# Turning half of the q tiles in 32x32 blocks on VectorE and through DRAM, and moving the output's addition and its LayerNorm sums to ScalarE and GpSimd

## The chip, the core and the metric

The kernel runs on one core of a Trainium2 chip. The metric is the device time of one execution in microseconds. A core has five instruction streams that matter here: TensorE (PE in the profile; its weight loads are listed apart as PEld), VectorE (DVE), ScalarE (ACT), GpSimd (POOL) and SyncE (SP), which here only issues DMA transfers. They run side by side and are ordered by semaphores alone: an instruction waits until a counter has reached a value, and everything behind it in its stream waits too.

## What is computed

Sixteen batches of x and ctx, each 128 channels by 1024 positions, in float32. First a linear attention between x and ctx, whose output is added to x, then a feed-forward part with a routed table of values:

```python
x = x + xattn(layernorm(x), ctx, ctx, Wq, Wk, Wv, Wo, bo, g)
x = x + ffn(layernorm(x), ...)

def xattn(q, k, v, ...):              # 8 heads of 64
    qh = softmax(Wq q, over the 64) * 64 ** -0.5
    kh = softmax(Wk k, over the 1024 positions)
    vh = Wv v
    context = einsum('hdn,hen->hde', kh, vh)
    out = Wo einsum('hde,hdn->hen', context, qh) + bo
    return out / max(norm over channels, 1e-12) * g * sqrt(128)
```

LayerNorm runs along the 1024 positions. The FFN part is computed from its sums, so the mean and variance of every row of the new x are needed before it begins.

## The kernel before

**Stages.** The attention stage runs the batches through a pipeline of periods, one batch a period, each of four steps (`for b in range(PERIODS): for i in range(4)`). In the loop, `b` is the batch whose k tiles are made, `p = b - 1` the one whose q tiles are made and whose context product is taken, `o = b - 2` the one whose output is taken, `e = b - 3` the one that is finished. Every engine has the same loop written out in its own block, in an order set by hand. After it comes the FFN stage, whose first steps are woven into the last periods.

**The k side.** `k_tile` (L444) makes four tiles of k with 1024 columns; VectorE takes a maximum (`k_maximum`, L1102), ScalarE the exponential (`k_exponential`, L734). The result has to be turned, so that the context product can contract over positions: VectorE transposes it in 32x32 blocks into `kt` (`k_turn`, L1106), and SP moves the blocks between partitions into `ekT`, in 2 halves of 16 DMAs of 64 KB for each batch (`move_k`, L377, issue in L384). `g_part` (L471) on TensorE waits until a half has landed. In the first batch GpSimd issues half of these DMAs.

**The q side.** `q_pair` (L453) makes four q tiles a batch, each of two groups of 128 positions. VectorE subtracts the maximum of each head (`q_shift`, L1120), ScalarE takes the exponential, VectorE the sums and reciprocals (`q_reciprocal`, L1130), GpSimd scales (`q_scale`, L966). The scaled tile lies in `qs_sb`, with two buffers. TensorE turns all four tiles with eight transpositions each into the PSUM tensor `turn` (`q_turn`, L462), ScalarE copies them to `q_hd` (`q_copy`, L750), and `o_pair` (L495) multiplies them with the batch's matrix `mt_sb`.

**The output.** ScalarE copies the products (`o_copy`), sums their squares (`o_square`), GpSimd scales by the norm (`norm_scale`, L978), TensorE turns the result into `turn` (`o_turn`, L510). VectorE adds it to x in one operation (`residual`, L1141) and takes the row statistics (`statistics`, L1146: two `bn_stats` of 512 columns and an aggregation). GpSimd makes the reciprocal deviation (`rstd2_pow`, L987). `turn` is shared: whoever uses it next on TensorE waits for the copy of the one before (`take_turn`, L615).

**SP's order.** In the loop of L401 SP issues, for batch b: the load of x for b + 1, the first half of `move_k`, the loads of ctxT for b and of ctx for b + 2, the second half of `move_k`. After the loop come the small tables of the FFN stage. Each block of moves waits for the two transposes of its half and for the `g_part` that last read the buffer.

Of the kernel before, what the change touches and what calls it, by code (L numbers as in the profile page):

```python
# [25 lines left out]
MOVED = 16 * QUAD * QUAD  # L26
LN_EPS = 1e-5
# [15 lines left out]
def place(h):  # L43

    return (h % 2) * (H // 2) + h // 2


def attention_ffn_kernel(nc, x, ctx_rows, ctx_cols, WqT_raw, WkT_raw, Wv_rows, WoT_rows, bo_row, g_col, Wuq_cols,
# [3 lines left out]
    with ctx:  # L52
# [19 lines left out]
        q_hd = sb("q_hd", [P, T, N])  # L72
        qs_sb = sb("qs_sb", [P, 2, N])
        mt_sb = sb("mt_sb", [P, 2, T, C])
# [11 lines left out]
        kscale = sb("kscale", [P, T])  # L86
# [4 lines left out]
        mv1 = sb("mv1", [P, 2])  # L91
# [24 lines left out]


# [151 lines left out]
        kscale_done = sem("kscale_done")  # L269
# [14 lines left out]
        q_copied = sem("q_copied")  # L284

# [78 lines left out]
        def _(sp):  # L364
# [22 lines left out]

            sp.dma_start(WkT_in, WkT_raw).then_inc(k_weights_in, 16)
# [22 lines left out]
            for half in range(2):  # L411
                sp.wait_ge(k_moved[half], moved(B))
            sp.dma_start(bu1[:, :], bu1_row.broadcast_to([P, UH])).then_inc(ffn_in, 16)
            sp.wait_ge(q_prod, 4 * B)
            sp.wait_ge(g_prod, 2 * B)
            sp.wait_ge(m_prod, B)
            for src, dst in ((Wu2_row.broadcast_to([P, UH]), Wu2[:, :]),
                             (bu2_row.broadcast_to([P, 1]), bu2[:, :]),
                             (gate_w_row.broadcast_to([P, 1]), gate_w[:, :]),
                             (gate_b_row.broadcast_to([P, 1]), gate_b[:, :])):  # L420
                sp.dma_start(dst, src).then_inc(ffn_in, 16)
            sp.dma_start(WvuT_in[:, :], WvuT_raw).then_inc(wvu_in, 16)
# [14 lines left out]
        def _(pe):  # L437
# [57 lines left out]
            def o_pair(b, i):  # L495
                pe.wait_ge(q_copied, 4 * b + i + 1)
# [6 lines left out]
                for j in (2 * i, 2 * i + 1):  # L503
                    for t in range(T):
                        last = nc.tensor.matmul(ob[:, (j % 4) * C:(j % 4 + 1) * C],  # L505
                                                q_hd[:, t, j * P:(j + 1) * P], mt_sb[:, b % 2, t, :],
                                                start=(t == 0), stop=(t == T - 1))
                last.then_inc(o_prod, 1)

            def o_turn(b):  # L510
                pe.wait_ge(o_scaled, b + 1)
                for j in range(J):
                    last = nc.tensor.transpose(turn[:, j * P:(j + 1) * P], o_sb[:, b % 2, j, :], ident[:, :])  # L513
# [98 lines left out]
            copies = {q_turn: (q_copied, 4), o_turn: (x1_done, 1)}  # L612
            used = []

            def take_turn(user, b, i=0):  # L615
                if used:
                    before, n = used.pop()
                    pe.wait_ge(copies[before][0], n)
                used.append((user, copies[user][1] * b + i + 1))

            pe.wait_ge(k_weights, 2)
            for b in range(PERIODS):
                p, o, e = b - 1, b - 2, b - 3
                for i in range(4):
# [8 lines left out]
                    if has(qb):  # L633
                        if qb == 0 and qi == 0:
# [81 lines left out]
        def _(act):  # L716
# [33 lines left out]
            def q_copy(b, i):  # L750
                act.wait_ge(q_T, 4 * b + i + 1)
                wait(act, o_prod, 4 * (b - 1) + i + 1)
                nc.scalar.copy(q_hd[:, :, 2 * i * P:2 * (i + 1) * P],  # L753
                               turn[:, :].rearrange("p (t n) -> p t n", t=T)).then_inc(q_copied, 1)

            def o_copy(b, half):
                act.wait_ge(o_prod, 4 * b + 2 * (half + 1))
                wait(act, o_T, b - 1)
# [4 lines left out]
            def o_square(b, half):  # L763
# [3 lines left out]
                wait(act, o_T, b)  # L767
                for j in range(4 * half, 4 * half + 4):
                    last = nc.scalar.activation(o_sb[:, (b + 1) % 2, j, :], o_sb[:, b % 2, j, :], ACT.Square,
                                                accum_out=l2[:, j:j + 1])  # L770
                last.then_inc(l2_sum, 1)

            def mt_scale(b):
                act.wait_ge(m_prod, b + 1)
                act.wait_ge(kscale_done, b + 1)
# [659 lines left out]
```

## Time and profile before

| | |
|---|---|
| median of 3 runs | 639.78 us (639.23 to 642.43) |
| span of the profiled execution | 638.0 us |
| TensorE busy | 618.3 us, 97% |
| VectorE busy | 540.5 us, 85% |
| ScalarE busy | 416.7 us, 65% |
| GpSimd busy | 371.8 us, 58% |
| DMA moved | 72.57 MB, 114 GB/s in the mean |

The span is that of one profiled execution, which is where all durations below come from; the page gives no other time for it, and the median of the runs is 1.8 us above it. A busy share is an average over the whole span: the attention stage goes to about 500 us, the FFN stage fills the rest. The issuing of DMAs is not counted as busy, so SP has no share of its own in the page; its timeline has to be asked for. Operations that follow each other on one engine overlap a little, so the sum of their durations is somewhat more than the time that they take together.

### The profile page before, as it was taken

What the parts mean: (1) busy time and instruction counts of PE and PEld (TensorE: products, weight loads), DVE (VectorE), ACT (ScalarE), POOL (GpSimd) and SP (SyncE); (2) the same over time, 40 slices, a digit from 0 to 9 for tenths busy, and PEclk for the clock granted to TensorE, in tenths of its full rate; (3) what the DMA queues carried; (4) which work ended last, traced back from release to release, by engine and by line L of the source; (5) the groups of instructions that cost most, each with busy time, mean ns of one, the idle gap of its engine ahead of it and who ended that gap; (6) DMA issues with size and microseconds to landing.
All of it is one profiled execution on the core that took longest, in us unless ns stands there. A gap on an engine that the chain in (4) does not pass through costs nothing.

```text
span 638.0 us, 11806 instructions
## 1 busy us (share of the span) xinstructions
PE 618.3 (97%) x3974; PEld 543.1 (85%) x3974; DVE 540.5 (85%) x757; ACT 416.7 (65%) x844; POOL 371.8 (58%) x369
## 2 busy tenths in 40 slices
PE   4999999999999999999999999999999999999896
PEld 3778888888898888888898888888888999998674
DVE  5989898998989898989898989898986844756897
ACT  5566666666676666667676766666664767674693
POOL 4954474847474747474757575665646446520394
PEclk9999999999999999999999999999999999999799
DMA  8944543444444444444445344433344100000056
GB/s 299 242 116 108 144 110 117 120 125 114 126 112 124 110 133 114 126 116 121 111 129 161 102 124 113 134 104 96 79 120 126 42 2 1 2 1 1 34 230 265
DMA packets 52010, 72.57 MB, mean 114 GB/s; under 512 B 10112, under 2 KB 42400, under 8 KB 51696
## 3 DMA queue, kind: packets, MB, share of 16 engines
q1 hardware_dynamic: 50912, 68.07, 37.1%
q0 software_dynamic: 896, 2.45, 1.2%
q10 hardware_dynamic: 144, 1.31, 0.6%
q8 instruction: 32, 0.52, 0.4%
q14 instruction: 26, 0.21, 0.1%
HBM read 29.85 MB, written 8.39 MB: 60 GB/s over the span
## 4 chain that ended last, share of the span: by engine, by line
PE 91%; DMA 3%; SPq 2%; DVE 1%; issue 1%; ACT 1%; POOL 0%; DVEq 0%; ACTq 0%; POOLq 0%
PE ob L505 18%; PE gm L482 17%; PE turn L466 8%; PE gm L558 4%; PE k_slot L440 4%; PE q_slot L440 4%; PE q_slot L442 4%; PE k_slot L442 4%; PE q_slot L441 4%; PE k_slot L441 4%; PE turn L558 4%; PE gm L491 2%; PE turn L513 2%; SPq L384 2%; DMA x_all<-Wvd_cols 1%; PE turn L682 1%
## 5 line engine op out<-in xcount | busy, mean ns | idle before, releaser
L969 POOL TENSOR_TENSOR qs_sb<-qs_sb,qrec 128x1024 f32<-128x1024 f32 x64 | 122.0, 1906 | 148.9 <-DVE qrec L1139 148.9
L738 ACT ACTIVATE ek<-k_slot,nkm 128x1024 f32<-128x1024 f32 x62 | 69.1, 1114 | 94.6 <-DVE nkm L1104 94.5
L505 PE MATMUL ob<-mt_sb,q_hd 128*128 128x128 f32 x1024 | 126.4, 277 | 0.6 <-ACT o_sb L760 0.5
L505 PEld LDWEIGHTS ob<-mt_sb,q_hd 128*128 128x128 f32 x1024 | 121.8, 192 | 5.2 <-issue 3.6
L482 PE MATMUL gm<-ekT,ctxT 128*128 128x256 f32 x512 | 118.2, 379 | 1.1 <-DMA ekT<-kt 1.1
L482 PEld LDWEIGHTS gm<-ekT,ctxT 128*128 128x128 f32 x512 | 97.0, 190 | 16.2 <-DMA ekT<-kt 1.5
L748 ACT ACTIVATE qs_sb<-qs_sb 128x1024 f32<-128x1024 f32 x64 | 68.6, 1071 | 31.7 <-DVE qs_sb L1128 31.7
L1104 DVE TENSOR_REDUCE nkm<-k_slot 128x1 f32<-128x1024 f32 x62 | 74.2, 1197 | 14.8 <-PE k_slot L442 14.7
L1135 DVE TENSOR_REDUCE qsum<-qs_sb 128x16 f32<-128x1024 f32 x64 | 76.9, 1202 | 4.1 <-ACT qs_sb L748 4.1
L1128 DVE TENSOR_TENSOR qs_sb<-q_slot,qm 128x1024 f32<-128x1024 f32 x64 | 78.4, 1224 | 2.2
L1111 DVE STREAM_TRANSPOSE kt<-ek 128x1024 f32<-128x1024 f32 x64 | 78.5, 1227 | 0.6 <-DMA ekT<-kt 0.6
L1125 DVE TENSOR_REDUCE qm<-q_slot 128x16 f32<-128x1024 f32 x64 | 75.6, 1181 | 0.0
L466 PEld LDWEIGHTS turn<-ident,qs_sb 128*128 128x128 f32 x512 | 59.6, 140 | 8.1 <-issue 0.5
L466 PE MATMUL turn<-ident,qs_sb 128*128 128x128 f32 x512 | 66.3, 272 | 0.0
L753 ACT COPY q_hd<-turn 128x1024 f32<-128x1024 f32 x64 | 64.3, 1005 | 2.9 <-PE turn L466 2.9
L440 PE MATMUL k_slot<-ctx_hi,WkT_hi 128*128 128x512 f32 x124 | 54.7, 441 | 8.3 <-DVE ctx_lo L1289 7.4
L440 PE MATMUL q_slot<-WqT_hi,xn_hi 128*128 128x512 f32 x128 | 55.7, 435 | 0.0
L442 PE MATMUL q_slot<-WqT_lo,xn_hi 128*128 128x512 f32 x128 | 50.5, 395 | 0.0
L441 PE MATMUL q_slot<-WqT_hi,xn_lo 128*128 128x512 f32 x128 | 49.9, 390 | 0.0
L442 PE MATMUL k_slot<-ctx_lo,WkT_hi 128*128 128x512 f32 x124 | 49.3, 398 | 0.0
L441 PE MATMUL k_slot<-ctx_hi,WkT_lo 128*128 128x512 f32 x124 | 49.1, 396 | 0.0
L963 POOL TENSOR_TENSOR xn_lo<-xn,xn_hi 128x1024 fp32r<-128x1024 f32 x16 | 38.3, 2396 | 14.7 <-ACT xn_hi L732 14.7
(200 smaller groups left out, 1231.9 us busy)
## 6 DMA issues: line engine op xcount, KB each, us to landing
ekT<-kt SPq DMA_DIRECT2D x496, 64.0 KB, 2.0
ctx_in<-ctx_rows SPq DMA_DIRECT2D x16, 512.0 KB, 4.6
x_all<-x SPq DMA_DIRECT2D x16, 512.0 KB, 3.6
ctxT<-ctx_cols SPq DMA_DIRECT2D x16, 512.0 KB, 4.1
out<-q_hd SPq DMA_DIRECT2D x15, 512.0 KB, 2.6
Wuq_in<-Wuq_cols ACTq DMA_DIRECT2D x1, 1280.0 KB, 6.5
x_all<-values_cols POOLq DMA_DIRECT2D x1, 1024.0 KB, 8.3
ekT<-kt POOLq DMA_DIRECT2D x16, 64.0 KB, 4.3
```

The source lines that it names most:

```text
L440: nc.tensor.matmul(dst, lhs[0], rhs[0], start=True, stop=False)
L441: nc.tensor.matmul(dst, lhs[1], rhs[0], start=False, stop=False)
L442: return nc.tensor.matmul(dst, lhs[0], rhs[1], start=False, stop=True)
L466: last = nc.tensor.transpose(turn[:, (2 * t + n) * P:(2 * t + n + 1) * P], qs_sb[:, i % 2, n * HALF + t * P:n * HALF + (t + 1) * P], ident ...
L482: last = nc.tensor.matmul(gm[:, cols], ctxT[:, b % 2, j, :], ekT[:, 2 * half:2 * half + 2, :, j * BLK:(j + 1) * BLK], start=(j == 0), stop ...
L505: last = nc.tensor.matmul(ob[:, (j % 4) * C:(j % 4 + 1) * C], q_hd[:, t, j * P:(j + 1) * P], mt_sb[:, b % 2, t, :], start=(t == 0), stop=( ...
L969: nc.gpsimd.tensor_tensor(e, e, qrec[:, i % 2, :].unsqueeze(2).broadcast_to([P, PAIR, DH]), ALU.mult).then_inc(q_mul, 1)
L1104: V.tensor_reduce(nkm[:, i:i + 1], k_psum(b, i)[:, :], AX, ALU.max, negate=True).then_inc(k_max, 1)
L1111: V.transpose(kt[:, i, :], ek[:, i % 2, :]).then_inc(k_T, 1)
L1125: V.tensor_reduce(qm[:, :], q, AX, ALU.max).then_inc(q_max, 1)
L1128: V.tensor_tensor(qs_sb[:, i % 2, :].rearrange("p (m d) -> p m d", d=DH), q, qm[:, :].unsqueeze(2).broadcast_to([P, PAIR, DH]), ALU.subtra ...
L1135: V.tensor_reduce(qsum[:, :], qs_sb[:, i % 2, :].rearrange("p (m d) -> p m d", d=DH), AX, ALU.add).then_inc(q_sum, 1)
```

## The change

1. Of the four q tiles of a batch, tiles 0 and 2 are turned by TensorE as before. Tiles 1 and 3 are transposed by VectorE in 32x32 blocks into a new tensor `qt` (`q_block_turn`), written by SP to DRAM (`q_out`, one DMA of 512 KB) and read back into `q_hd` with the blocks moved between partitions (`q_in`, four DMAs of 128 KB). `q_block_turn` stands on VectorE ahead of `q_shift`, two steps after its tile was made. SP waits between the two for the write to land. `o_pair` reads these tiles with the head pairs as the innermost dimension. Since the positions of such a tile come in another order, `o_turn` writes its columns back in place.
2. `q_hd` holds one row of 1024 columns a tile, instead of a slice of each head pair.
3. For the first 13 batches the output's scaling goes to ScalarE (`o_scale`, which also sums it), the addition to x to GpSimd (`residual` in GpSimd's block, in step 0 of the next period, ahead of `q_scale`), the sum of squares about the mean to ScalarE (`square_sum`). `rstd2_pow` forms the variance from it and stands at the end of the period. Batches 13 to 15 keep the operations on VectorE.
4. The factor 64 ** -0.5 goes from `kscale` into the matrix U, once; the scaling of `krec` in each batch goes away.
5. The squares of `o_square` are written to a tensor of their own (`junk`), and the scratch space for GpSimd's DMAs is 4096 bytes.

The diff, cut to its core:

```diff
+BY_BLOCKS = (1, 3)
+BY_PE = tuple(i for i in range(4) if i not in BY_BLOCKS)
+RESIDUAL_BY_VECTOR = B - 3
...
+            def q_out(b, i):
+                n = BY_BLOCKS.index(i)
+                sp.wait_ge(q_blocks, len(BY_BLOCKS) * b + n + 1)
+                wait(sp, q_back[n], 16 * QUAD * (b - 1))
+                sp.dma_start(q_turned[b % 2, n].rearrange("p q x -> p (q x)"), qt[:, n, :]).then_inc(q_written[n], 16)
+
+            def q_in(b, i):
+                n = BY_BLOCKS.index(i)
+                sp.wait_ge(q_written[n], 16 * (b + 1))
+                wait(sp, o_prod, 4 * (b - 1) + i + 1)
+                for q in range(QUAD):
+                    sp.dma_start(q_hd[q * BLK:(q + 1) * BLK, i, :].rearrange("r (a x) -> r a x", a=QUAD),
+                                 q_turned[b % 2, n, :, q, :].rearrange("(a r) x -> r a x", a=QUAD)).then_inc(q_back[n], 16)
...
-            for b in range(B):
+            for b in range(B + 1):
                 if 2 <= b + 1 < B:
                     load_x(b + 1)
-                move_k(b, 0)
-                if b >= 2:
+                if has(b):
+                    move_k(b, 0)
+                for i in (0, 1):
+                    if i in BY_BLOCKS and has(b - 1):
+                        q_out(b - 1, i)
+                if 2 <= b < B:
                     load_ctxT(b)
                 if 2 <= b + 2 < B:
                     load_ctx(b + 2)
-                move_k(b, 1)
+                for i in (0, 1):
+                    if i in BY_BLOCKS and has(b - 1):
+                        q_in(b - 1, i)
+                if has(b):
+                    move_k(b, 1)
+                else:
+                    ffn_tables()
+                for i in (2, 3):
+                    if i in BY_BLOCKS and has(b - 1):
+                        q_out(b - 1, i)
+                for i in (2, 3):
+                    if i in BY_BLOCKS and has(b - 1):
+                        q_in(b - 1, i)
...
             def o_pair(b, i):
-                pe.wait_ge(q_copied, 4 * b + i + 1)
+                if i in BY_BLOCKS:
+                    pe.wait_ge(q_back[BY_BLOCKS.index(i)], 16 * QUAD * (b + 1))
+                else:
+                    pe.wait_ge(q_copied, turned_by_pe(b, i))
...
+                by_pe = q_hd[:, i, :].rearrange("p (t n x) -> p t n x", t=T, n=2)
+                by_blocks = q_hd[:, i, :].rearrange("p (n x t) -> p t n x", t=T, n=2)
...
             def o_turn(b):
...
+                    if j // 2 in BY_BLOCKS:
+                        cols = tile.rearrange("p (n h a x) -> p h a n x", n=2, h=2, a=2)[:, j % 2, :, :, :]
...
+            def o_scale(b):
+                act.wait_ge(o_T, b + 1)
...
+                nc.scalar.activation(o_sb[:, b % 2, :, :].rearrange("p j c -> p (j c)"), turn[:, :], ACT.Copy,
+                                     scale=gs[:, :], accum_out=osum[:, b % 2:b % 2 + 1]).then_inc(o_back, 1)
+
+            def square_sum(b):
+                act.wait_ge(x1_done, b + 1)
+                act.wait_ge(nm2_done, b + 1)
...
+                nc.scalar.activation(o_sb[:, b % 2, :, :].rearrange("p j c -> p (j c)"), X[:, b, :], ACT.Square,
+                                     bias=nm2[:, b % 2:b % 2 + 1], accum_out=ssq[:, :]).then_inc(ssq_done, 1)
...
+            def residual(b):
+                pool.wait_ge(o_back, b + 1)
+                nc.gpsimd.tensor_tensor(X[:, b, :], X[:, b, :], o_sb[:, b % 2, :, :].rearrange("p j c -> p (j c)"),
+                                        ALU.add).then_inc(x1_done, 1)
+                nc.gpsimd.tensor_scalar(mv2[:, b, 0:1], osum[:, b % 2:b % 2 + 1], 1.0 / N, mv1[:, b, 0:1], ALU.mult,
+                                        ALU.add).then_inc(mean2_done, 1)
...
+                nc.gpsimd.tensor_scalar(nm2[:, b % 2:b % 2 + 1], mv2[:, b, 0:1], -1.0, None,
+                                        ALU.mult).then_inc(nm2_done, 1)
...
+            def q_block_turn(b, i):
+                n = BY_BLOCKS.index(i)
+                dve.wait_ge(q_mul, 4 * b + i + 1)
+                wait(dve, q_written[n], 16 * b)
+                V.transpose(qt[:, n, :].rearrange("p (m x t) -> p m t x", m=QUAD * 2, t=T),
+                            qs_sb[:, i % 2, :].rearrange("p (m q x) -> p q m x", q=QUAD, m=2 * T)).then_inc(q_blocks, 1)
...
-                V.tensor_scalar_mul(kscale[:, :], krec[:, :], float(DH) ** -0.5).then_inc(kscale_done, 1)
...
-                    if i == 2 and has(e):
+                    if i == 2 and has(e) and e >= RESIDUAL_BY_VECTOR:
                         residual(e)
-                    if i == 3 and has(e):
+                    if i == 3 and has(e) and e >= RESIDUAL_BY_VECTOR:
                         statistics(e)
...
-    nc = bacc.Bacc("TRN2", target_bir_lowering=False, num_devices=1)
+    nc = bacc.Bacc("TRN2", target_bir_lowering=False, num_devices=1, dynamic_dma_scratch_size=4096)
```

## Rows read from the trace of the kernel before

**Rows 1.** The page: busy time of each engine; the chain that ended last, by engine.

```profile
PE 618.3 (97%) x3974; PEld 543.1 (85%) x3974; DVE 540.5 (85%) x757; ACT 416.7 (65%) x844; POOL 371.8 (58%) x369
...
PE 91%; DMA 3%; SPq 2%; DVE 1%; issue 1%; ACT 1%; POOL 0%; DVEq 0%; ACTq 0%; POOLq 0%
```

**Rows 2.** SP's timeline, one period: start us, duration, line, operation, number merged.

```profile
323.04 11.12 SPq L384 DMA_DIRECT2D ekT<-kt  x16
334.20 0.58 SPq L375 DMA_DIRECT2D x_all<-x  x1
336.75 10.17 SPq L384 DMA_DIRECT2D ekT<-kt  x16
346.97 0.58 SPq L372 DMA_DIRECT2D ctxT<-ctx_cols  x1
347.65 0.40 SPq L368 DMA_DIRECT2D ctx_in<-ctx_rows  x1
353.79 10.18 SPq L384 DMA_DIRECT2D ekT<-kt  x16
```

**Rows 3.** One period as a window: length, busy PE..POOL, clock, DMA share, GB/s.

```profile
323.04:353.79 30.75, 30.75 (x201) 27.16 (x200) 28.15 (x34) 20.30 (x42) 19.26 (x19) 1.00 0.43 121
```

**Rows 4.** All of SP's move issues: duration in ns, min/median/max.

```profile
L384 SPq DMA_DIRECT2D ekT<-kt x496: 585/597/1776, 17.1 to 487.5; - x166
```

**Rows 5.** TensorE's timeline: a q turn, the next product, the last g_part.

```profile
321.95 1.04 PE L466 MATMUL turn<-ident,qs_sb 128*128 128x128 f32 x8
322.74 0.47 PE L440 MATMUL q_slot<-WqT_hi,xn_hi 128*128 128x512 f32 x1
...
489.56 3.72 PE L482 MATMUL gm<-ekT,ctxT 128*128 128x256 f32 x16 [1.10 <-DMA ekT<-kt]
```

**Rows 6.** VectorE's timeline: statistics, a block transpose, the residual.

```profile
320.38 1.27 DVE L1150 BATCH_NORM_STATS2 st<-x_all 128x6 f32<-128x512 f32 x2
321.69 0.21 DVE L1152 BATCH_NORM_AGGREGATE mv<-st 128x2 f32<-128x12 f32 x1
...
329.19 1.23 DVE L1111 STREAM_TRANSPOSE kt<-ek 128x1024 f32<-128x1024 f32 x1
...
343.05 1.28 DVE L1143 SCALAR_TENSOR_TENSOR x_all<-turn,gs,x_all 128x1024 f32<-128x1024 f32 x1 [1.47 <-PE turn L513]
```

**Rows 7.** Groups by line, 300 to 420 us: ScalarE's exponential, GpSimd's norm scale.

```profile
L748 ACT ACTIVATE qs_sb<-qs_sb 128x1024 f32<-128x1024 f32 x15 | 16.1, 1074 | 5.6 <-DVE qs_sb L1128 5.6
...
L984 POOL TENSOR_TENSOR o_sb<-o_sb,rn 128x1024 f32<-128x1024 f32 x4 | 7.6, 1896 | 0.3
```

**Rows 8.** SP's timeline: blocks of moves of batch 1, the next, the last.

```profile
33.81 10.17 SPq L384 DMA_DIRECT2D ekT<-kt  x16
...
47.53 10.88 SPq L384 DMA_DIRECT2D ekT<-kt  x16
...
61.24 11.42 SPq L384 DMA_DIRECT2D ekT<-kt  x16
...
476.74 11.39 SPq L384 DMA_DIRECT2D ekT<-kt  x16
```

**Rows 9.** The page's DMA issues: KB each, median us from issue to landing.

```profile
ekT<-kt SPq DMA_DIRECT2D x496, 64.0 KB, 2.0
...
x_all<-x SPq DMA_DIRECT2D x16, 512.0 KB, 3.6
...
out<-q_hd SPq DMA_DIRECT2D x15, 512.0 KB, 2.6
```

**Rows 10.** Groups by line: the weight loads of o_pair, busy us and mean ns.

```profile
L505 PEld LDWEIGHTS ob<-mt_sb,q_hd 128*128 128x128 f32 x1024 | 121.8, 192 | 5.2 <-issue 3.6
```

**Rows 11.** Windows of 2 us in the FFN stage, columns as in rows 3.

```profile
590.00:592.00 2.00, 0.54 (x2) 0.29 (x2) 1.97 (x8) 0.96 (x5) 0.00 (x0) 0.86 0.00 0
592.00:594.00 2.00, 1.54 (x7) 1.42 (x7) 1.11 (x6) 1.03 (x4) 0.00 (x0) 0.50 0.00 0
...
598.00:600.00 2.00, 2.00 (x12) 1.39 (x10) 1.04 (x4) 1.24 (x3) 0.00 (x0) 0.93 0.00 0
```

More of the change, by code:

```diff
@@ L284, in attention_ffn_kernel @@
         q_copied = sem("q_copied")
+        q_blocks = sem("q_blocks")
+        q_written = [sem(f"q_written{i}") for i in BY_BLOCKS]
+        q_back = [sem(f"q_back{i}") for i in BY_BLOCKS]
+        o_back = sem("o_back")
+        mean2_done = sem("mean2_done")
+        nm2_done = sem("nm2_done")
+        ssq_done = sem("ssq_done")
         o_prod = sem("o_prod")
@@ L502, in o_pair @@
                     wait(pe, o_copied, 2 * b + i // 2)
-                for j in (2 * i, 2 * i + 1):
+                by_pe = q_hd[:, i, :].rearrange("p (t n x) -> p t n x", t=T, n=2)
+                by_blocks = q_hd[:, i, :].rearrange("p (n x t) -> p t n x", t=T, n=2)
+                for n in range(2):
+                    j = 2 * i + n
                     for t in range(T):
-                        last = nc.tensor.matmul(ob[:, (j % 4) * C:(j % 4 + 1) * C],
-                                                q_hd[:, t, j * P:(j + 1) * P], mt_sb[:, b % 2, t, :],
+                        q = (by_blocks if i in BY_BLOCKS else by_pe)[:, t, n, :]
+                        last = nc.tensor.matmul(ob[:, (j % 4) * C:(j % 4 + 1) * C], q, mt_sb[:, b % 2, t, :],
                                                 start=(t == 0), stop=(t == T - 1))
@@ L512, in o_turn @@
                 for j in range(J):
-                    last = nc.tensor.transpose(turn[:, j * P:(j + 1) * P], o_sb[:, b % 2, j, :], ident[:, :])
+                    tile = turn[:, (j // 2) * 2 * P:(j // 2 + 1) * 2 * P]
+                    if j // 2 in BY_BLOCKS:
+                        cols = tile.rearrange("p (n h a x) -> p h a n x", n=2, h=2, a=2)[:, j % 2, :, :, :]
+                    else:
+                        cols = tile[:, (j % 2) * P:(j % 2 + 1) * P]
+                    last = nc.tensor.transpose(cols, o_sb[:, b % 2, j, :], ident[:, :])
                 last.then_inc(o_T, 1)
@@ L608, in hidden_step @@
                         score(n)
-            copies = {q_turn: (q_copied, 4), o_turn: (x1_done, 1)}
             used = []
@@ L616, in take_turn @@
                 if used:
-                    before, n = used.pop()
-                    pe.wait_ge(copies[before][0], n)
-                used.append((user, copies[user][1] * b + i + 1))
+                    copied, n = used.pop()
+                    pe.wait_ge(copied, n)
+                if user is q_turn:
+                    used.append((q_copied, turned_by_pe(b, i)))
+                elif b < RESIDUAL_BY_VECTOR:
+                    used.append((o_back, b + 1))
+                else:
+                    used.append((x1_done, b + 1))
             pe.wait_ge(k_weights, 2)
@@ L632, in _ @@
                     qb, qi = (p, i - 2) if i >= 2 else (o, i + 2)
-                    if has(qb):
-                        if qb == 0 and qi == 0:
+                    if has(qb) and qi in BY_PE:
+                        if qb == 0 and qi == BY_PE[0]:
                             pe.wait_ge(u_done, 1)
@@ L848, in _ @@
                     qb, qi = (p, i - 2) if i >= 2 else (o, i + 2)
-                    if has(qb):
-                        if qb == 0 and qi == 0:
+                    if has(qb) and qi in BY_PE:
+                        if qb == 0 and qi == BY_PE[0]:
                             act.wait_ge(k_weights, 2)
@@ L857, in _ @@
                         o_square(o, 0)
+                    if i == 3 and 0 <= e < RESIDUAL_BY_VECTOR:
+                        o_scale(e)
                     if i == 1 and 0 < b < B:
                         x_layernorm(b)
+                    if i == 1 and 0 <= e - 1 < RESIDUAL_BY_VECTOR:
+                        square_sum(e - 1)
                     if i == 2:
@@ L1035, in _ @@
                         mt_bias(o)
+                    if i == 0 and 0 <= e - 1 < RESIDUAL_BY_VECTOR:
+                        residual(e - 1)
                     if i == 3 and 0 < b < B:
@@ L1044, in _ @@
                         rstd_pow(b)
-                    if i == 0 and has(e - 1):
+                    if i == 0 and has(e - 1) and e - 1 >= RESIDUAL_BY_VECTOR:
+                        rstd2_pow(e - 1)
+                    if i == 3 and 0 <= e - 1 < RESIDUAL_BY_VECTOR:
                         rstd2_pow(e - 1)
@@ L1315, in _ @@
                             k_scale(p)
+                    qb, qi = (p, i - 2) if i >= 2 else (o, i + 2)
+                    if has(qb) and qi in BY_BLOCKS:
+                        q_block_turn(qb, qi)
                     if has(p):
                         q_shift(p, i)
-                    if i == 2 and has(e):
+                    if i == 2 and has(e) and e >= RESIDUAL_BY_VECTOR:
                         residual(e)
-                    if i == 3 and has(e):
+                    if i == 3 and has(e) and e >= RESIDUAL_BY_VECTOR:
                         statistics(e)
```

86 lines of the change are left out of this document (53 added, 33 removed).

## The prediction

> **What bounds the kernel now.** I read the page's busy shares and chain first. TensorE is busy for 97% of the span and carries 91% of the chain [rows 1], so over the whole kernel it sets the time. Then I looked at one period of the attention stage, one batch, found from SP's timeline: the same block of DMA issues begins at 323.04 and again at 353.79, so a period is 30.75 us [rows 2]. The window table of exactly that stretch shows TensorE busy for all of it, VectorE for 28.15, ScalarE for 20.30, GpSimd for 19.25 [rows 3]. VectorE has only 2.6 us of slack, the others have about ten.
>
> The table of busy times does not count an engine that issues DMAs, so SP's timeline has to be read by itself [rows 2]. In the period SP issues two blocks of 16 `move_k` DMAs (11.12 and 10.17 us), one load of x, one of ctxT, one of ctx. A single one of these moves holds SP for 0.60 us (median) [rows 4]; with the gap it is 10.17/16 = 0.64. SP waits only from 334.78 to 336.75 and from 348.05 to 353.79: 7.7 us of 30.75. So SP is about 75% occupied, and it is the queue into which the change puts ten more DMAs and two more waits per batch.
>
> **What the change takes and adds, engine by engine, for one period.**
>
> TensorE loses two of four `q_turn`s. From the start of one to the start of the next product is 322.74 - 321.95 = 0.79 us [rows 5], so 2 x 0.79 = 1.6 us go and TensorE needs 29.2. The two tiles' output products remain, only their operand is laid out differently.
>
> VectorE loses `residual` (1.28), the two `bn_stats` (1.27 together), one aggregation (0.21) and the tiny kscale; it gains two block transposes. A transposition of the same size takes 1.23 [rows 6]. 28.15 - 2.76 + 2.46 = 27.9. It stays below TensorE's 29.2.
>
> ScalarE loses two copies of 1.0 and gains `o_scale` and `square_sum`; the nearest row for a pass over 128x1024 is 1.07 [rows 7]. That is about +0.4 with the two reads of the sums, taken at nothing: ten us of slack hide it. GpSimd gains an addition of 128x1024, 1.90 [rows 7], and three one-column operations, some 3 us in all, against 11.5 of slack. `residual` now stands ahead of the last `q_scale` of a batch, but what that `q_scale` feeds is read a step (over 7 us) later, so this too I cost at nothing; without that cover it would be 3 us per period. The smaller DMA scratch acts only on GpSimd's own DMAs in the first 28 us; it can't gain, and if it slowed them it would move the start by a few us; I take 0.
>
> SP gains, for each of the two tiles, one write of 512 KB to DRAM (`q_out`), a wait until that write has landed, and four reads of 128 KB back (`q_in`). Queued behind that wait on SP are the next 16 `move_k` DMAs, and TensorE's `g_part` waits for these. Neither the write nor the reads is in the trace. Their bounds:
> - A read, four 1 KB runs in each of 32 partitions, is nearest to a `move_k` DMA (two such runs). The 26 blocks of 16 that stand alone between 61 and 489 us (first and last: [rows 8]) take 10.79 by the mean of the 26, so 0.67 for one; some of the sixteen take longer than the median. The plain ctx load issued in 0.40 [rows 2] is the lower end. I take 0.67: 4 x 0.67 = 2.7 for one tile.
> - The write, from issue to landing: a store of 512 KB lands after 2.6 us where little else runs, a load of the same size after 3.6 in this stage, a 64 KB move after 2.0 [rows 9]. I take 3.0, since a write is a store but follows right behind sixteen moves; ends 2.0 and 3.6. Its own issue lies inside this time. For tile 1 the ctxT and ctx issues (1.1 us) lie inside it too, so they cost nothing any more.
>
> One round of SP is then 2 x 10.79 (moves) + 0.6 (x) + 2 x 3.0 (landing) + 2 x 2.7 (reads) = 33.6 us, against 30.75 now and 29.2 that TensorE would need. SP becomes the bound of the attention stage: it has 7.7 us to spare and is given 11.4 - 1.1 = 10.3, and its moves are counted at their mean. At 33.6 does anything else make SP wait besides? I laid the events of one round after one another. A block of moves for the second half of ekT ends at 0; its last piece lands 1.4 later and releases `g_part`. TensorE then needs about one step, a quarter of 30.75, until the fourth k tile is through, and VectorE three operations of some 1.2 us and a reciprocal more to the block transpose that the next `q_out` of tile 1 wants: ready at 1.4 + 7.7 + 3.9 = 13. SP has tile 3's round trip, the x load and the first half of the moves in front of it, 5.7 + 0.6 + 10.8 = 17.1. So it does not wait, with 4 us over.
>
> On the way in, the block (b=1, half 0) is issued from 33.81 to 43.98 [rows 8]; a transposition (1.2), landing (3.0), reads (2.7) put the start of (1, half 1) at 50.9 instead of 47.53. From there fourteen rounds lead to the last block, (15, half 1): 50.9 + 14 x 33.6 = 521.3. Now it begins at 476.74 [rows 8]: +44.6. TensorE already waits for exactly this block (1.10 us before 489.56 [rows 5]), so what comes later there comes later in the end. The block itself took 11.39 there and takes 10.8 on average: -0.6. In what follows two more `q_turn`s fall away, -1.6; tile 3's last round trip lands, by the order of the steps, some 3 us before its product. Sum +42.4: the span of 638.0 becomes 680.4, and with the 1.8 by which the median of the runs (639.78) exceeds that span, **682**.
>
> **Where the skill disagrees.** The trace gives an issue of 0.60 us against 2.0 to landing, and SP 75% occupied [rows 2, 4, 9]. The Trainium skill ("DMA: Bandwidth & Descriptors", section "Issuing engines are not separate DMA queues") calls the sequencer's time to start a DMA "usually small relative to the DMA itself". By that rule the ten new DMAs would cost SP next to nothing; that is rival 1 below. The trace doesn't bear it out for the moves.
>
> **Rivals.**
> 1. *SP stays below TensorE: faster.* If reads issued like the ctx load, 8 x 0.40 = 3.2, moves at their floor, 2 x 10.17, and the write landed like a small move, 2 x 2.0, SP's round is 20.3 + 0.6 + 4.0 + 3.2 = 28.1. Then TensorE's 29.2 decides: 15 x -1.6 = -24, **616**. For it: VectorE, ScalarE and GpSimd do have the room. Against: all three must hold at once, and [rows 2, 9] show them only for smaller or simpler DMAs. It decides as soon as SP's round is under 29.2.
> 2. *Break-even.* A round of 30.5 to 31, between the two, moves the time by less than 0.5%, about 637 to 643; 0.5% is about what a measurement of this kernel can tell from no change.
> 3. *Strided operands.* The new tiles have their four head pairs innermost, so the weight load of 32 of the 64 `o_pair` instructions reads every fourth float. No row shows such a load. A contiguous one occupies 121.8/1024 = 0.12 us [rows 10]; if a strided one takes twice that, TensorE needs 29.2 + 32 x 0.12 = 33.0. Under SP's 33.6 this is hidden. If SP is fast after all, it is the bound: 15 x 2.25 = +34, **674**. The block transposes write with the same stride: 2.46 more would bring VectorE to 30.3, hidden by both. The Trainium skill ("SBUF — State Buffer", section "Door 1: The DMA port swizzle") says that accesses which go to a new 16-byte line each time pay a penalty; it gives no price for this case, and no row here shows one.
> 4. *TensorE's clock.* SP's delay opens gaps of some 3 us ahead of `g_part`. In the FFN stage TensorE, busy for 0.54 of 2.0 us, went from a granted 1.00 to 0.50 (2.4 to 1.2 GHz) for about 6.8 us: 0.86 in the first window, 0.50 in three, 0.93 in the last [rows 11]. One such drop per period costs 3.4, 32.6 in all, still under SP. Two would make 36.0: 14 x 2.4 = +34 on the forecast, **716**.
>
> **How the numbers follow.** Forecast (SP's round of 31.4 to 34.8, that is 14 x -2.2 and 14 x +1.2: 651 to 699) 0.72; rival 1 0.08; rival 2 0.05; rival 3 0.07; rival 4 0.08. Faster 0.08, same 0.05, slower 0.87. The range 648 to 716 leaves out rivals 1 and 2 and about the outer part of the forecast and of rival 4, near 0.2.
>
> **What would show it.** In the changed kernel's period: SP's timeline without pauses other than the two for the landing write; TensorE idle for about 4 us per period, put down to the DMA into ekT, ahead of `g_part`; the period near 33.6; VectorE no busier per batch than now. A `g_part` that never waits for ekT, or SP waiting for VectorE's k transposes as it does now, would refute the forecast. Weight loads of `o_pair` well above 0.12 and no SP stall would point to rival 3, a granted clock under 0.9 to rival 4.

## The result, and the profile after

The changed kernel takes 676.97 us (676.31 to 677.15), the kernel before 640.45 in the same comparison: a ratio of 1.056, 95% interval 1.051 to 1.061. The forecast was 682 with a range of 648 to 716. The sum held; the mechanism that it was put down to did not. TensorE hardly waits for SP. It is busy all the time, with weight loads that became twice as long, which is rival 3.

The page after: busy times, the chain by engine, the groups of `o_pair` (now line 565), and the DMA issues.

```profile
PE 649.6 (96%) x3718; PEld 575.1 (85%) x3718; DVE 563.3 (83%) x721; ACT 421.8 (62%) x864; POOL 409.7 (61%) x421
...
PE 88%; DVE 3%; DMA 3%; SPq 2%; issue 2%; ACT 1%; POOL 0%; DVEq 0%; ACTq 0%; POOLq 0%
...
L565 PE MATMUL ob<-mt_sb,q_hd 128*128 128x128 f32 x1024 | 187.3, 336 | 1.5 <-issue 1.0
L565 PEld LDWEIGHTS ob<-mt_sb,q_hd 128*128 128x128 f32 x1024 | 182.8, 260 | 6.0 <-issue 4.5
...
q_turned<-qt SPq DMA_DIRECT2D x32, 512.0 KB, 2.9
q_hd<-q_turned SPq DMA_DIRECT2D x128, 128.0 KB, 3.1
```

Against [rows 1], TensorE executes 256 instructions fewer (the turns that went) and is busy for 31 us more. Against [rows 10], the weight loads of `o_pair` occupy 182.8 us instead of 121.8. Half of the 1024 are unchanged at 0.119, so each of the other half takes (182.8 - 512 x 0.119)/512 = 0.238 us, twice as much.

SP's timeline after, one period (columns as in [rows 2]; a block that the answer's end cuts off is not shown):

```profile
314.19 11.00 SPq L404 DMA_DIRECT2D ekT<-kt  x16
325.30 0.53 SPq L413 DMA_DIRECT2D q_turned<-qt  x1
328.15 1.74 SPq L421 DMA_DIRECT2D q_hd<-q_turned  x4
329.93 0.43 SPq L395 DMA_DIRECT2D x_all<-x  x1
330.46 10.55 SPq L404 DMA_DIRECT2D ekT<-kt  x16
341.81 0.34 SPq L413 DMA_DIRECT2D q_turned<-qt  x1
342.19 0.43 SPq L392 DMA_DIRECT2D ctxT<-ctx_cols  x1
342.72 0.66 SPq L388 DMA_DIRECT2D ctx_in<-ctx_rows  x1
344.82 1.75 SPq L421 DMA_DIRECT2D q_hd<-q_turned  x4
```

The next period begins at 346.67: 32.48 us here. The second blocks of batch 1 and of batch 15 are these:

```profile
52.48 10.22 SPq L404 DMA_DIRECT2D ekT<-kt  x16
...
510.37 11.84 SPq L404 DMA_DIRECT2D ekT<-kt  x16
```

Over the fourteen rounds between them the mean is (510.37 - 52.48)/14 = 32.71, before (476.74 - 47.53)/14 = 30.66 [rows 8]. This mean, taken from the same two blocks, is called the round below. SP is now occupied almost throughout. The window table of this period, columns as in [rows 3], and TensorE's timeline inside it:

```profile
314.19:346.67 32.48, 32.48 (x183) 29.15 (x184) 28.61 (x31) 20.54 (x45) 21.78 (x22) 1.00 0.60 173
```

```profile
315.95 1.95 PE L565 MATMUL ob<-mt_sb,q_hd 128*128 128x128 f32 x16
317.65 0.48 PE L493 MATMUL k_slot<-ctx_hi,WkT_hi 128*128 128x512 f32 x1
...
322.21 3.79 PE L565 MATMUL ob<-mt_sb,q_hd 128*128 128x128 f32 x16
325.75 0.48 PE L493 MATMUL k_slot<-ctx_hi,WkT_hi 128*128 128x512 f32 x1
```

TensorE is busy for all of the 32.48 us. Tile 0, turned by TensorE, takes 1.70 from its start to that of the next product; tile 1, which came by blocks, takes 3.54. Two such tiles make +3.68 per period; less the 1.58 of the turns [rows 5], 30.66 becomes 32.76. Measured 32.71. What SP waits for, in 100 to 500 us (total, times, longest):

```profile
SPq L421 <- DMA q_turned<-qt: 44.9, 24, 2.6
SPq L413 <- DVE qt L1256: 10.1, 14, 1.1
```

The second line, which the forecast did not have, is the reserve that SP still has: 0.80 us in the period shown (from 341.01 to 341.81). Without it SP's round is about 31.7, one microsecond under TensorE's. The two bounds lie close together: the ctxT load, issued behind SP's wait, lands less than 1 us ahead of the first `g_part` that reads it in twelve of the fourteen rounds, and in the first and the last TensorE waits 0.46 and 0.39 us for it.

### The profile page after: what moved, and what is told of

Its sections match the earlier page's. It is cut to its first block, busy times and chain, and to the rows that moved or that the text cites. A ratio compares the mean times of both kernels' runs of the same rounds, so it can differ in the third digit from the quotient of the medians.

```text
span 675.3 us, 11559 instructions
## 1 busy us (share of the span) xinstructions
PE 649.6 (96%) x3718; PEld 575.1 (85%) x3718; DVE 563.3 (83%) x721; ACT 421.8 (62%) x864; POOL 409.7 (61%) x421
## 2 busy tenths in 40 slices
DMA packets 75051, 106.12 MB, mean 157 GB/s; under 512 B 12672, under 2 KB 61344, under 8 KB 74736
## 4 chain that ended last, share of the span: by engine, by line
PE 88%; DVE 3%; DMA 3%; SPq 2%; issue 2%; ACT 1%; POOL 0%; DVEq 0%; ACTq 0%; POOLq 0%
PE ob L565 25%; PE gm L535 16%; PE gm L622 4%; PE q_slot L493 4%; PE q_slot L495 4%; PE k_slot L493 4%; PE q_slot L494 4%; PE k_slot L495 4%; PE k_slot L494 4%; PE turn L519 4%; PE turn L622 4%; PE gm L544 2%; PE turn L577 2%; SPq L404 2%; DMA x_all<-Wvd_cols 1%
## 5 line engine op out<-in xcount | busy, mean ns | idle before, releaser
L1059 POOL TENSOR_TENSOR qs_sb<-qs_sb,qrec 128x1024 f32<-128x1024 f32 x64 | 121.8, 1903 | 137.4 <-DVE qrec L1249 137.4
L565 PE MATMUL ob<-mt_sb,q_hd 128*128 128x128 f32 x1024 | 187.3, 336 | 1.5 <-issue 1.0
L565 PEld LDWEIGHTS ob<-mt_sb,q_hd 128*128 128x128 f32 x1024 | 182.8, 260 | 6.0 <-issue 4.5
L1256 DVE STREAM_TRANSPOSE qt<-qs_sb 128x1024 f32<-128x1024 f32 x32 | 65.9, 2061 | 0.0
L493 PE MATMUL q_slot<-WqT_hi,xn_hi 128*128 128x512 f32 x128 | 53.4, 417 | 2.0 <-DVE qs_sb L1238 2.0
L838 ACT ACTIVATE junk<-o_sb 128x128 f32<-128x128 f32 x128 | 37.8, 301 | 0.0
L1036 POOL TENSOR_TENSOR ctx_lo<-ctx_in,ctx_hi 128x1024 fp32r<-128x1024 f32 x15 | 35.7, 2377 | 1.0 <-ACT ctx_hi L788 1.0
```

The costliest lines, as they stand in the source:

```text
L493: nc.tensor.matmul(dst, lhs[0], rhs[0], start=True, stop=False)
L1059: nc.gpsimd.tensor_tensor(e, e, qrec[:, i % 2, :].unsqueeze(2).broadcast_to([P, PAIR, DH]), ALU.mult).then_inc(q_mul, 1)
```

## The experiments

Rounds are read from SP's timeline as above. Ratios are against the kernel before on the same chip (639.3 to 641.0 us by median). "Values mixed" means that the positions or head pairs of some q tiles are wrongly assigned, so that only the time counts.

| kernel | us | ratio (95%) | round, us |
|---|---|---|---|
| before | 640.45 | | 30.66 |
| changed | 676.97 | 1.056 (1.051 to 1.061) | 32.71 |
| ScalarE reads back | 680.51 | 1.062 (1.055 to 1.068) | 32.68 |
| consecutive loads | 671.80 | 1.048 (1.041 to 1.054) | 32.34 |
| both of these | 658.47 | 1.027 (1.019 to 1.035) | 31.49 |
| SP's load alone | 671.43 | 1.047 (1.042 to 1.052) | 32.90 |
| output part alone | 643.26 | 1.004 (1.000 to 1.008) | 30.56 |
| all consecutive | 634.77 | 0.993 (0.990 to 0.995) | 29.97 |
| head pairs outermost | 721.71 | 1.126 (1.119 to 1.133) | 35.41 |
| stride two | 641.58 | 1.005 (1.002 to 1.009) | 30.36 |
| stride two, reordered | 625.68 | 0.977 (0.974 to 0.980) | 29.10 |

**SP relieved.** The four reads of each tile and the wait ahead of them go to ScalarE.

```diff
-                sp.wait_ge(q_written[n], 16 * (b + 1))
+                act.wait_ge(q_written[n], 16 * (b + 1))
...
-                    sp.dma_start(q_hd[q * BLK:(q + 1) * BLK, i, :].rearrange("r (a x) -> r a x", a=QUAD),
+                    nc.scalar.dma_start(q_hd[q * BLK:(q + 1) * BLK, i, :].rearrange("r (a x) -> r a x", a=QUAD),
```

> The changed kernel with its eight reads back per batch (q_in) issued and waited for by ScalarE instead of SP; SP keeps the two writes. All values stay the same. Theory W (TensorE's strided weight loads set the period of 32.6 us): 674 to 680 us, period 32.6, TensorE busy throughout, o_pair of tiles 1 and 3 still 3.5 us each, SP idle for 8 to 9 us per period. Theory S (SP's round sets it, and the slow loads only fill time that TensorE would have waited): SP's round falls from about 31.7 to about 23, the period to 29 to 30.5, the time to 620 to 645.

680.51, not faster. SP's waits, and all engines in the window from 150 to 480:

```profile
SPq L404 <- DVE kt L1216: 43.6, 20, 2.5
SPq L413 <- DVE qt L1252: 43.5, 20, 3.7
```

```profile
150.00:480.00 330.00, 330.00 (x1860) 295.26 (x1859) 293.26 (x304) 213.57 (x448) 224.41 (x235) 1.00 0.61 176
```

SP now has 87 us of waits in ten periods, 8.7 each, and the round is the same. So SP is not needed to explain the time: the forecast's mechanism falls, TensorE with its strided loads is a bound by itself.

**Loads relieved.** `o_pair` reads 128 consecutive floats in tiles 1 and 3 as well; values mixed.

```diff
-                by_blocks = q_hd[:, i, :].rearrange("p (n x t) -> p t n x", t=T, n=2)
...
-                        q = (by_blocks if i in BY_BLOCKS else by_pe)[:, t, n, :]
+                        q = by_pe[:, t, n, :]
```

> The changed kernel, but o_pair reads tiles 1 and 3 with 128 consecutive floats per weight load, as tiles 0 and 2, so that in these tiles positions and head pairs are mixed up: work and waits are the same, the values of these tiles are not the reference's. Theory W: o_pair of these tiles falls from 3.5 to 1.7 us, TensorE needs 29.0 per period; SP's own round of about 31.7 is what is left as the bound: 660 to 666 us, TensorE waiting about 2.5 us per period for the DMA into ekT. Theory S: the period stays at 32.6 and the time at 674 to 680, the TensorE time that is freed turning into waiting.

671.80: only 5 us back, where 660 to 666 was expected from the strided loads. All four tiles take 1.95 to 2.05 now, yet the round falls by 0.4 only. SP waits for little but its landings, and TensorE waits once per period, ahead of the first half of `g_part`:

```profile
SPq L421 <- DMA q_turned<-qt: 38.0, 20, 2.7
SPq L413 <- DVE qt L1255: 4.0, 5, 1.2
```

```profile
307.19 0.34 SPq L392 DMA_DIRECT2D ctxT<-ctx_cols  x1
```

```profile
ctxT<-ctx_cols SPq DMA_DIRECT2D x1, 512.0 KB, 4.5
```

```profile
311.79 1.96 PE L535 MATMUL gm<-ekT,ctxT 128*128 128x256 f32 x8 [2.60 <-issue]
```

The profile names no releaser ("issue"), but the ctxT load that this product needs is issued at 307.19, behind `q_out`'s wait, and lands 4.5 later, at 311.7, just before the product starts. It is so in all fourteen rounds: the product begins within 0.15 us of this landing, after a wait of 0.7 to 3.2 us, 1.7 in the mean of the ten from 150 to 480. So there is a second bound nearly as high as the first: SP's round, in which the forecast had the right engine and the wrong victim. What comes late is not the block of moves but the ctxT load behind the same wait.

**Both relieved.** Values mixed as above.

> Both edits: consecutive floats in the weight loads of tiles 1 and 3 (values of these tiles not the reference's) and the reads back issued by ScalarE. Theory W with SP as the second bound: neither is left; VectorE with its 2.06 us block transposes (about 29.4 per period) or TensorE (29.0) decides: 618 to 635 us. If the time stays above 650, a third bound is there that neither theory names.

658.47: 18.5 us gained, about a third of what was expected. TensorE still waits for ctxT (it is issued behind the wait for the block transposition), 0.5 to 1.2 us in every round, and for VectorE's `q_shift`, about 1 us a round. VectorE is busy for 305 of 330 us; its block transposition takes 2.07 us where the k turn of the same size takes 1.23 [rows 6].

**SP's load alone.** The kernel before with everything on TensorE and VectorE as it was; SP only carries two tiles a batch to DRAM and back into a tensor that nobody reads. ScalarE's copy of these tiles also has to wait until the write of the batch before has landed, but no such wait shows from 150 to 480 us.

```diff
-                sp.wait_ge(q_blocks, len(BY_BLOCKS) * b + n + 1)
+                sp.wait_ge(q_copied, turned_by_pe(b, i))
...
-                    sp.dma_start(q_hd[q * BLK:(q + 1) * BLK, i, :].rearrange("r (a x) -> r a x", a=QUAD),
+                    sp.dma_start(qt[q * BLK:(q + 1) * BLK, n, :].rearrange("r (a x) -> r a x", a=QUAD),
```

> The work of the kernel before (all four q tiles turned by TensorE, consecutive floats in the weight loads, addition and statistics on VectorE) with the changed kernel's load on SP added: after ScalarE's copy of tiles 1 and 3, SP writes 512 KB to DRAM, waits for it and reads it back into a tensor that nobody uses. If SP's round is a bound of its own, as plain_loads showed (about 32.4 us per period with 16 more slow issues at times), the period grows from 30.75 to about 32.4: 655 to 668 us, TensorE waiting 1.5 to 2 us per period ahead of g_part. If SP's load only mattered together with the rest of the change: 638 to 644 us.

671.43, +31 us, a little above the 655 to 668 expected. The largest waits of TensorE's products and of SP (150 to 480):

```profile
PE gm L535 <- issue: 16.8, 8, 4.8
```

```profile
SPq L421 <- DMA q_turned<-q_hd: 41.6, 20, 4.3
SPq L413 <- ACT q_hd L816: 7.0, 4, 4.7
```

This is nearly the forecast's case in pure form: SP full, TensorE with gaps ahead of `g_part`, the round 32.90. The gaps are 1.7 us a round in the mean, not 4, and they too end with ctxT's landing, not with that of the moves. One of the fourteen rounds takes 37.15: ctxT lands after 7.2 us in it, TensorE's granted clock is 0.50 from 346 to 352 us, and SP waits 4.7 us for ScalarE's copy; the mean of the others is 32.57. SP's price was estimated well; it just isn't added to TensorE's, the two run side by side.

**The price of a stride.** The work of the kernel before; the weight loads of tiles 0, 1, 2 and 3 read every 2nd, 3rd, 4th and 8th float (values mixed).

```diff
+                step = (2, 3, 4, 8)[i]
...
+                        q = q_hd[:, i, first:first + step * (P - 1) + 1:step]
```

> As the kernel before in its work (all four q tiles turned by TensorE, no DRAM round trip, output's addition on VectorE), but q_hd kept by tile and the weight loads of o_pair reading every 2nd, 3rd, 4th and 8th float for tiles 0, 1, 2, 3; positions and head pairs are mixed up and the values are not the reference's. It measures the price of a strided weight load by itself. Theory W: tile 2 takes 3.5 us as in the changed kernel against 1.7 for consecutive floats. If the price comes once a 16-byte line is read for one float only, tile 0 stays at 1.7, tile 1 lies between, tile 3 is again 3.5: 640 + 15.5 x 4.3 = about 705 us. If it grows with the stride, tile 0 is already slower and tile 3 the slowest, near 7. Theory S: tile 2 stays near 1.7 here, since no engine keeps TensorE waiting.

TensorE's timeline, the four tiles of one batch in the order 1, 2, 3, 0:

```profile
306.68 2.89 PE L534 MATMUL ob<-mt_sb,q_hd 128*128 128x128 f32 x16
...
317.38 3.90 PE L534 MATMUL ob<-mt_sb,q_hd 128*128 128x128 f32 x16
...
325.88 4.08 PE L534 MATMUL ob<-mt_sb,q_hd 128*128 128x128 f32 x16
...
335.17 2.04 PE L534 MATMUL ob<-mt_sb,q_hd 128*128 128x128 f32 x16
```

The kernel took 716.75 in one run. Without a stride tiles 0 to 2 take 1.95 and tile 3, which follows another product, 2.05. Stride 2 is nearly free, stride 3 costs 0.9 for sixteen loads, 4 and 8 about 2.0 each. Together that is 5.0 us a batch; by the expectation's own sum 640 + 15.5 x 5.0 = 718, near the 716.75. The Trainium skill ("SBUF — State Buffer", section "Door 1: The DMA port swizzle") says that accesses are at full rate when at least two fall into the same 16-byte line. The ladder agrees: at stride 2 two floats of each line are read, 2.04 us, from 4 on one, 3.90 and 4.08. The ladder adds the price.

**The output part alone.** All four tiles by TensorE; only the output's scaling, addition and sums go to ScalarE and GpSimd. The small points of the change, `q_hd` by tile, the factor in U, `junk` and the scratch space, are in it too.

> Only the output part of the change: o_scale, residual and square_sum on ScalarE and GpSimd for 13 batches, all four q tiles turned by TensorE, no DRAM round trip; o_scale stands at the end of step 2 on ScalarE, since turn is needed by the next tile. TensorE's work is that of the kernel before, and it was busy throughout; VectorE loses 2.8 us per period. Expected: 637 to 645 us, no change beyond 0.5%. If the way over ScalarE and GpSimd holds turn longer than VectorE's one operation did, TensorE waits ahead of the q turn of step 3: 650 or more.

643.26, ratio 1.004 with 1.000 in its interval: no change that can be told. It takes VectorE from 301.6 to 273.6 us of work in 330, and TensorE stays at 330: the freed time lies beside the bound. In the changed kernel the pieces cost what was taken or a little more: GpSimd's addition 2.40 us (1.90 taken), ScalarE's two passes 1.10 and 1.14 (1.07 taken), all hidden.

**All consecutive.** Consecutive loads and a transposition that writes consecutively (values mixed), the reads on ScalarE, the ctxT load ahead of the moves.

> The changed kernel with every cost that the runs named taken away: consecutive floats in the weight loads and in the writes of the block transposes of tiles 1 and 3 (their values are then not the reference's), the reads back issued by ScalarE, and the load of ctxT issued ahead of the moves instead of behind the wait of q_out. TensorE needs 29.2 per period, VectorE about 27.8, SP about 24: 612 to 628 us. If it stays above 640, the block turn has a cost that was not found.

634.77, above the 612 to 628 expected. The transposition takes 1.20 instead of 2.06 us. No wait for ctxT is left, but two others are:

```profile
294.51 0.47 PE L478 MATMUL q_slot<-WqT_hi,xn_hi 128*128 128x512 f32 x1 [0.78 <-DVE qs_sb L1233]
```

```profile
310.88 1.22 DVE L1208 TENSOR_REDUCE nkm<-k_slot 128x1 f32<-128x1024 f32 x1 [2.15 <-PE k_slot L480]
```

TensorE waits for VectorE to empty the single q buffer, and a few steps on VectorE waits for TensorE. Neither is full; they hold each other up.

**Head pairs outermost.** Another layout with consecutive loads; the tile goes to DRAM in four writes, in runs of 256 bytes, and comes back in one read on ScalarE.

> The same idea with all values kept: VectorE turns the tile in two instructions of 512 columns and writes consecutive floats, SP writes each tile with four DMAs of 256-byte runs into a DRAM layout in which the head pairs come first, ScalarE reads it back with one DMA of 4 KB rows, o_pair reads consecutive floats, ctxT is loaded ahead of the moves. If runs of 256 bytes cost the DMA engines little, as plain_all: 612 to 632 us, below the kernel before. If they land so late that o_pair or the next moves wait, 640 to 680, with TensorE waiting for the DMA into q_hd or ekT.

721.71, above both expected ranges. TensorE's waits, the DMA packets, and the window from 150 to 480 here and in the version all consecutive:

```profile
PE ob L551 <- DMA q_hd<-q_turned: 34.6, 14, 4.7
```

```profile
DMA packets 123820, 106.13 MB, mean 147 GB/s; under 512 B 77824, under 2 KB 110112, under 8 KB 123504
```

```profile
150.00:480.00 330.00, 291.83 (x1700) 252.63 (x1701) 256.76 (x296) 193.32 (x408) 205.50 (x219) 0.93 0.60 162
150.00:480.00 330.00, 321.22 (x2024) 278.45 (x2022) 300.12 (x326) 226.99 (x480) 243.01 (x251) 1.00 0.69 192
```

Of the packets 77824 are under 512 bytes (12672 in the changed kernel and in all consecutive). A `move_k` lands after 3.6 us by the median, against 2.1 in the changed kernel and 2.6 in all consecutive, and `q_hd` comes too late. TensorE's clock has a part in it as well: behind these waits it fell to 0.50 again and again, and the mean granted clock is 0.93 against 1.00. With rounds of 35.41 and 29.97, TensorE is busy for 31.3 us a round against 29.2 and idle for 4.1 against 0.8. So of the 5.4 us that a round is longer, some 2 go with the lower clock and some 3 with the waits. Single periods here reach 37.

**Stride two.** Every second float in the load, four writes in runs of 512 bytes, one read of 512 KB on ScalarE, ctxT ahead of the moves.

```diff
+                        if i in BY_BLOCKS:
+                            first = (t // 2) * 4 * P + n * 2 * P
+                            q = q_hd[:, i, first + t % 2:first + 2 * P:2]
...
+                for a in range(QUAD):
+                    sp.dma_start(q_turned[b % 2, n, :, :, :, a, :].rearrange("h q r y -> r (h q) y"),
+                                 qt[a * BLK:(a + 1) * BLK, n, :].rearrange("r (g y) -> r g y", y=4 * BLK)).then_inc(q_written[n], 16)
```

> A version of the change that computes the same outputs, with a layout meant to avoid what the earlier runs showed as costly: the weight loads of tiles 1 and 3 read every second float instead of every fourth, the tile goes to DRAM in runs of 512 bytes (four writes of 128 KB) and comes back in one read of 512 KB that ScalarE issues, and the ctxT load stands ahead of the moves. The block transposition takes four instructions of 256 columns, and they write every second float. If the stride of the load is what counts, o_pair of tiles 1 and 3 takes about 2.0 us for its 16 products instead of 3.8 to 4.0, and TensorE needs 29.3 us per period. VectorE: 28 to 29 of the period, if four pieces take 1.5 us where one consecutive transposition took 1.20. SP: 2 x 10.8 for the moves, 0.6 + 0.4 + 0.6 for the loads, 2 x 2.6 to 3.65 for the writes (what four writes took in the version with runs of 256 bytes), together 28.4 to 30.5. If nothing new appears: a period of 30 to 30.7, 635 to 645. If the runs of 512 bytes still slow the neighbouring transfers as those of 256 bytes did (the moves landed after 3.6 us there instead of 2.1, the period was 37), TensorE waits for q_hd and it comes out at 660 to 700. In no case under 632, which the version with consecutive loads left as its span.

641.58: of the 36.5 us by which the changed kernel is slower, 35 are gone. The sixteen loads of tiles 1 and 3 take 2.04 to 2.15 us, the round is 30.36, and the pair of waits of the version all consecutive remains (VectorE 2.1 us per period).

**Stride two, reordered.** One step is moved into that wait.

```diff
+                    if i == 3 and has(p) and 1 in BY_BLOCKS:
+                        q_block_turn(p, 1)
                     if 0 < b < B:
                         k_maximum(b, i)
```

> As the version with stride two, with one thing moved: on VectorE the block transposition of tile 1 stands ahead of the fourth k maximum instead of behind it. In the trace of the version with stride two VectorE waits there for 2.13 us per period (from 312.10 to 314.23, for k tile 3), and GpSimd has scaled tile 1 by 311.5, while the transposition (1.36 us) stands a little later in the chain that makes TensorE wait for q_sub. If that chain of VectorE and TensorE, with a single buffer for q, is the bound (period 30.36), the 1.36 us disappear in the wait: TensorE's 29.3 us are next, 29.2 to 29.6 per period, 14 or 15 periods, -11 to -17 us, that is 622 to 631. If SP or the landing of q_hd is the bound instead, nothing changes: 637 to 645. If the scaled tile comes later than the wait begins, the k maximum is delayed and the gain is under 5 us.

625.68, 2.3% faster than the kernel before. VectorE's timeline at the place, and a period as a window:

```profile
305.00 1.38 DVE L1257 STREAM_TRANSPOSE qt<-qs_sb 128x256 f32<-128x256 f32 x4
307.22 1.23 DVE L1212 TENSOR_REDUCE nkm<-k_slot 128x1 f32<-128x1024 f32 x1 [0.84 <-PE k_slot L482]
```

```profile
284.23:313.38 29.15, 29.15 (x186) 25.71 (x185) 28.00 (x37) 20.89 (x46) 22.17 (x24) 1.00 0.73 195
```

The transposition lies in the wait, which falls from 2.13 to 0.84, and TensorE is busy for the whole period again, at 29.15 us (327 of 330 us from 150 to 480). The forecast's 29.2 for TensorE without two turns was right; it is what the idea is worth once nothing else is in its way.

## Why the prediction held, and where it did not

The sum, term by term against the profile. It had +3.4 for the way in, fourteen rounds of 33.6 instead of 30.66 (+41.2) and -2.2 for the way out: +42.4 on the span. Measured: +4.95 (52.48 against 47.53), 14 x 2.05 = +28.7, +3.7 (from the last block to the end 164.93 against 161.26): +37.3. So the rounds were 12.5 us too much, the way in 1.6 and the way out 5.9 too little; the errors partly cancel, and the span was forecast 5 us too long. That the total came so close is in part luck: the round was taken from SP, while the engine that set it stood only in rival 3, whose 674 was the nearer number and whose chance was put at 0.07. In the way in, SP waits 2.6 us for the block transposition, which was taken at 1.2.

- **SP's round (33.6): the price was nearly right, its role was not.** Moves 21.55 (21.58 taken), landings 2.85 and 3.01 (3.0 taken). The term that was mis-sized is the read: 1.75/4 = 0.44 us, not 0.67, so 3.5 for both tiles instead of 5.4. The choice went to the nearest row by shape, `move_k`, although the lower end, a plain load at 0.40, was closer. With it SP has about 31.7, and 0.8 of waiting for the block transposition.
- **"So it does not wait, with 4 us over"** failed. SP does wait for VectorE, 0.80 us in the period shown. Counted from the end of a block of moves (325.19), SP comes after 15.8 us, not 17.1, and the block transposition is ready after 16.6 (at 341.78), not 13: ahead of it VectorE waited 3.56 us for TensorE's k tile.
- **Rival 3 was the case**: 33.0 forecast, 32.76 from the rows after, 32.71 measured. The doubling of the load that was only assumed is what the ladder shows for a stride of 4. It was called hidden "under SP's 33.6"; with the read at its measured price it is the bound by one microsecond, and by less in the runs (with TensorE relieved of its strides the round is still 32.34). The block transposition took 2.06 (1.23 in the sum, 2.46 in the rival).
- **The signs named at the end decide it.** TensorE idle by some 4 us ahead of `g_part` did not appear, weight loads well above 0.12 did. By the prediction's own test the likeliest case falls. In the way out, three strided tiles still follow the last `g_part` (at 532.46, 545.46 and 561.36 us, 3.86 to 4.00 each against 1.95 to 2.05). That is +5.8, which the sum left out and which is about what the way out was forecast too short.
- **Rival 1** (616, if SP were cheap) could not be had from SP alone: with SP relieved the time did not move, and with the strides, SP's reads and the late ctxT out of the way the q buffer holds the round at 29.97. It needed four changes together (loads at stride two, the reads on ScalarE, ctxT ahead, one step moved) to come to 625.68. Of the -11.7 between the two spans (626.3 and 638.0) the round gives 14 x -1.56 = -21.8; the way in (+4.1) and out (+5.9) take 10 us back. Of the way in, 2.7 lie ahead of the first block alone (36.48 against 33.81), with the clock at 0.50 from 22 to 28 us of this execution.
- **Rival 4**: in the changed kernel the granted clock is 1.00 in every window of 2 us from 50 to 540. TensorE had hardly a gap there, so the rival was not put to the test. Where other runs did open gaps ahead of `g_part`, the clock fell behind some of them: to 0.50 in four of the fourteen rounds with consecutive loads and in three with SP's load alone, for 3 to 4 us in most. So the mechanism exists here, and a part of those two times is the clock: with consecutive loads the four rounds take 32.83 us in the mean, the other ten 32.15.
- **The price of issuing** (rival 1's basis). In the period shown a read holds SP for 0.44 us and lands after 3.1 by the median, a move holds it for 0.67 and lands after 2.1. The Trainium skill ("DMA: Bandwidth & Descriptors", section "Issuing engines are not separate DMA queues") calls the time to start a DMA "usually small relative to the DMA itself". The trace agrees for the reads and less so for the moves. The 31 us of SP's load alone are those of ten more DMAs together with two waits for a landing on one queue; no run has the DMAs without the waits, so it does not refute that sentence.
- **Costed at nothing and confirmed**: the output part, by itself 1.004.

What is not settled: the wait for ctxT is read from its landing, in every round, and from its absence where the load was moved together with others; no run moved that load alone. How much of the 35 us between the changed kernel and stride two belongs to the stride, to the reads on ScalarE and to ctxT can't be divided, since any one bound left alone keeps most of the loss.

## What to carry to other kernels

When work is moved to other engines, check the layout that the moved data arrives in against whoever reads it: here the reader was the bound, by a small margin, and 32 loads of 0.12 us more cost more than the removed work gave. Several chains of nearly the same length must all be costed before one is called the cover of another, and a fix is judged only when all are relieved: each relief alone gave nothing or 5 us, all together 51. Then look for a wait on the engine that hands over last, and move a step into it.

## What had not been expected of the hardware

- Sixteen weight loads of 128x128 float32 with their products: 1.95 us consecutive, 2.04 at stride 2, 2.89 at 3, 3.90 at 4, 4.08 at 8. From 4 to 8 it hardly grows: the tile at 8 takes 2.05 without a stride.
- VectorE's transposition of 128x1024: 1.20 us with consecutive writes, 2.06 with writes 16 bytes apart; 1.36 to 1.40 in four pieces with writes 8 bytes apart.
- A DMA that reads four runs of 1 KB in each of 32 partitions from DRAM holds SP for 0.44 us, a move between partitions of half that size for 0.60.
- With writes to DRAM in runs of 256 bytes a 64 KB move beside them landed after 3.6 us. In runs of 512 bytes it was 2.6, the same as in the version all consecutive, whose writes have neither.
- TensorE's granted clock fell from 1.00 to 0.50 behind some of the waits ahead of `g_part` (consecutive loads: at about 84, 150, 215 and 409 us, after waits of 3.18, 1.91, 1.86 and 3.00), but not behind one of 2.60.
